# Second mixture: x stored to the output first, expert rows added onto it by the scatters, no closing stage

## The chip, the cores and the metric

The kernel runs on one core of one Trainium2 chip. The metric is the device time of one execution in microseconds; the time before is the median of three runs. A profile is of one execution. TensorE (PE), VectorE (DVE), ScalarE (ACT), Pool (GpSimd) and SP (SyncE) are the core's five engines; SP, ScalarE and Pool also issue the transfers (DMAs), which 16 DMA engines carry out.

## What is computed

3327 tokens of 256 features (padded to 26 tiles of 128 rows) go through four layers, each added onto `x`: a graph layer with an adjacency matrix, a mixture of experts, a second graph layer, and a transformer layer whose second half is another mixture. That last step is what the change is about:

```
def _moe(xf, ...):                      # capacity = ceil(T * 1.6 / 8)
    _, topk_idx = top_k(softmax(xf @ router_w + router_b), 2)
    out = zeros_like(xf)
    for i in range(8):
        sel = first `capacity` tokens that chose expert i
        hi = gelu(xf[sel] @ w1[i] + b1[i])
        out = out.at[sel].set(hi @ w2[i] + b2[i])     # a later expert overwrites
    return out
...
x = x + ctx @ wo + bo
h2 = layernorm(x)
return x + _moe(h2)
```

A token keeps the result of the last expert that took it, unweighted. A token that no expert took gets nothing. So each token has at most one expert row, and the result is `x` plus that row.

## The kernel before

The program is a list of blocks: first graph layer, routes and experts of the first mixture, second graph layer, attention, `second_norm`, routes and experts of the second mixture, and a closing block. All engines meet in a barrier at the end of each block; each engine first drains its own queue. Inside a block every engine has its instructions in the written order and waits on semaphores.

`second_norm` (line 1443) normalises `x` into `xhat`. SP stores `xhat` to `rows_d` in seven transfers (line 1559) and waits for them. Pool adds the kept `x` back onto `m.x` with seven transfers that add (line 1567, semaphore `back_added`); nothing in this block waits for these.

`mixture_routes` (line 638) is a chain of small VectorE operations: it picks the experts, ranks the tokens within each, and gives every token a slot among 20 chunks of 256 rows, each chunk of one expert. SP has nothing to do in it.

`expert_layers` (line 779) turns the slots into a list of token numbers (`index`, from which rows are gathered, and `place`, to which results go). Then, for each of the 20 chunks: Pool gathers 256 rows (two indirect transfers, line 1036), TensorE, ScalarE and VectorE compute the two layers with the chunk's weights, VectorE writes the result to one of two buffers `res` (line 1024), and Pool scatters it in two indirect transfers of 128 rows (line 1044). SP loads the weights two chunks ahead (line 841) and the biases (line 844). Pool's order in the loop is: gather chunk n+2, wait until the scatters of chunk n−1 landed and free that buffer (`release`), then wait for result n and scatter it. Slots without a token have a place of their own behind the 3328 rows.

The scatters write to `results1` in device memory. Tokens without an expert row must read zeros there, so Pool fills its first 3328 rows with zeros in the first graph layer (line 231, 13 transfers), behind the last use of the first four column groups of the adjacency matrix.

`mixture_output` (line 1068) is the closing block: SP reads the 3328 rows of `results1` in seven transfers (line 1079), VectorE multiplies each tile by the 0/1 weight of its tokens and adds it onto `x` (line 1087), ScalarE issues seven stores to `out` (line 1094) and waits for them.

Of the kernel before, what the change touches and what calls it, by code (L numbers as in the profile page):

```python
# [112 lines left out]
PIECE_RING = 4  # L113
RAW_RING = {True: 5, False: 4}
TOGETHER = 4
ZERO_TILES = 2
# [33 lines left out]
def graph_layer(nc, m, t, s, first):  # L150
# [38 lines left out]
    if first:  # L189
        made, params_loaded, x_loaded = s("made"), s("params_loaded"), [s(f"x_loaded{n}") for n in range(len(X_GROUPS))]  # L190
        rows_loaded, summed, reduced = [s("rows_loaded0"), s("rows_loaded1")], s("rows_summed"), s("rows_reduced")
        clamped, clamp_rooted = s("degree_clamped"), s("clamped_rooted")
        zero_made, rows_kept = s("zero_made"), s("rows_kept")
        m.pool_dma.append(rows_kept)
    else:
        wide_loaded, normed2, biased = s("qkv_loaded"), s("tiles_normed2"), s("bias_added")
        come, added = [s(f"row_come{n}") for n in range(GOT)], s("row_added")
        lifted = s("qk_lifted")
        x_kept, qk_kept, split = [s("x_kept0"), s("x_kept1")], [s("qk_kept0"), s("qk_kept1")], s("qk_split")
        m.pool_dma.extend(qk_kept + come)  # L200
    with ExitStack() as ctx:
# [9 lines left out]
        xt = sb("xt", [P, 2, KT, P])  # L211
        if first:
            adj_rows = m.xhat[:].rearrange("p t d -> p (t d)").rearrange("p (r n) -> p r n", r=2)
            zeros, iota_i, deg_tmp = sb("zeros", [P, ZERO_TILES, D]), sb("iota_i", [P, P], I32), sb("deg_tmp", [P, 2, NT])
# [9 lines left out]
        def _(pool):  # L224
            if first:
                make_constants(pool, m, iota_i, made)
                pool.memset(zeros[:], 0.0).then_inc(zero_made, 1)
                pool.wait_ge(zero_made, 1)
                pool.wait_ge(used, PIECES * TOGETHER)
                for n in range(0, NT, ZERO_TILES):  # L230
                    pool.dma_start(m.results1[0:NP, :].rearrange("(p n) d -> p n d", p=P)[:, n:n + ZERO_TILES, :], zeros[:]).then_inc(rows_kept, 16)
                for c in range(CHUNKS):
                    at = slice(first_tile(c), first_tile(c + 1))
                    pool.wait_ge(normed, at.stop)
                    pool.dma_start(m.rows_d[at.start * P:at.stop * P, :].rearrange("(k p) d -> p k d", p=P), m.xhat[:, at, :]).then_inc(rows_kept, 16)
# [399 lines left out]
            dve.wait_ge(chain, NT)  # L635


def mixture_routes(nc, m, s, bias, top, capacity, chunks, slot_sets, weights, idle_pool=None):

# [3 lines left out]
    with ExitStack() as ctx:  # L643
# [132 lines left out]

def expert_layers(nc, m, t, s, layer, chunks, n_rows, results):

# [20 lines left out]
    with ExitStack() as ctx:  # L801
# [229 lines left out]
        def _(pool):  # L1031
# [33 lines left out]
            release(chunks - 1)  # L1065


def mixture_output(nc, m, s, results, weight, x, out, x_whole):

    come, added, put = [s(f"results_come{c}") for c in range(CHUNKS)], s("results_added"), s("out_stored")
    with nc.sbuf_tensor(named("got"), [P, NT, D], F32) as got, nc.Block() as block:  # L1073

        @block.sync
        def _(sp):
            for c in range(CHUNKS):
                at = slice(first_tile(c), first_tile(c + 1))
                sp.dma_start(got[:, at, :], results[at.start * P:at.stop * P, :].rearrange("(k p) d -> p k d", p=P)).then_inc(come[c], 16)  # L1079

        @block.vector
        def _(dve):
            dve.wait_ge(*x_whole)
            for c in range(CHUNKS):
                dve.wait_ge(come[c], 16)
                for k in chunk_tiles(c):
                    dve.scalar_tensor_tensor(x[:, k, :], got[:, k, :], weight[:, k:k + 1], x[:, k, :], ALU.mult, ALU.add).then_inc(added, 1)  # L1087

        @block.scalar
        def _(act):  # L1090
            for c in range(CHUNKS):
                at = slice(first_tile(c), first_tile(c + 1))
                act.wait_ge(added, at.stop)
                act.dma_start(out[:, at, :], x[:, at, :]).then_inc(put, 16)
            act.wait_ge(put, 16 * CHUNKS)


def mixture(nc, m, t, s, layer, bias, capacity, chunks, results, out, idle_pool=None, x_whole=None):
    n_rows = TOP_K if capacity is None else 1
    mixture_routes(nc, m, s, bias, TOP_K, capacity, chunks, [(m.put[:, n, :], m.gets[n]) for n in range(n_rows)], m.weights, idle_pool)  # L1100
    expert_layers(nc, m, t, s, layer, chunks, n_rows, results)
    if out is not None:
        mixture_output(nc, m, s, results, m.weights[0], m.x, out, x_whole)


KEYS = 512
# [464 lines left out]
def second_mixture(nc, m, t, s, out):  # L1571

    back_added = second_norm(nc, m, s)
    mixture(nc, m, t, s, 1, m.bias8[:, 1, :], CAPACITY, MOE1_CHUNKS, m.results1, out, x_whole=(back_added, 16 * CHUNKS))


class Memory:


    def __init__(self, nc, ctx):  # L1580
# [23 lines left out]

        self.put = sb("put", [P, TOP_K, NT], I32)
        self.rows_d = dram("moe_rows", [NP, D])
        self.results0, self.results1 = dram("results0", [MOE0_CHUNKS * CHUNK, D]), dram("results1", [NP + MOE1_CHUNKS * CHUNK, D])
        self.x_kept, self.qk = dram("x_kept", [P, NT * D]), dram("qk_parts", [2, 2 * HG, P, NP])


def program(nc, t, out, phases="gnn0 moe0 gnn1 att moe1"):
    NAMES.clear()
    with ExitStack() as ctx:
# [15 lines left out]
        graph_layer(nc, m, t, s, True)  # L1629
        if "moe0" in phases:  # L1630
            _, s = stage()
            mixture(nc, m, t, s, 0, m.bias8[:, 0, :], None, MOE0_CHUNKS, m.results0, None,
                    idle_pool=lambda: nc.clear_and_free_semaphores([x for x in first if x not in m.pool_dma]))
        if "gnn1" in phases:
            _, s = stage()
# [56 lines left out]
```

## Time and profile before

| | us |
|---|---|
| median of three runs | 2770.12 |
| lowest, highest | 2769.33, 2773.91 |
| profiled execution, own time | 2769.95 |
| its span, first to last instruction | 2768.2 |
| busy in the span: TensorE | 2464.8 (89%) |
| busy in the span: VectorE, ScalarE, Pool | 2011.6, 1573.0, 1275.3 |
| second norm and routes | about 2407 to 2479 |
| experts of the second mixture | about 2479 to 2746 |
| closing block | 2746.0 to 2768.2 |

The page gives the busy time of each engine and 40 slices of the span. The last slice, 69 us long, shows TensorE at 5 tenths and the DMA engines at 4; slices are too coarse for the question here, so the rows below come from timelines and from the instructions of single lines. Queue instructions (DRAIN, EVENT_SEMAPHORE) belong to an engine's sequencer, marked by a q behind the engine's name.

### The profile page before, as it was taken

To read this page: it belongs to the slowest core of one execution; us is meant where nothing else is said; L and a number is where in the kernel's file an instruction comes from. 1 tells how busy PE (TensorE), PEld (TensorE's weight loads), DVE (VectorE), ACT (ScalarE), POOL (GpSimd) and SP (SyncE) were. 2 spreads that over 40 slices of the span, in tenths; PEclk is the share of its full clock that TensorE was granted. 3 is DMA by queue.
4 is the path that set the end of the run, shared out by engine and by line. 5 is a ranking of instruction groups with operands and counts; after the bars stand their busy time and mean duration, and the time that the engine had idled before them with its cause. 6 is when DMAs were issued, how large, how long until landed. Compare 5 with 4: busy or idle time off the path is not lost. (4 is left out here: it accounts for less than half of the span.)

```text
span 2768.2 us, 54324 instructions
## 1 busy us (share of the span) xinstructions
PE 2464.8 (89%) x20834; PEld 1910.6 (69%) x20834; DVE 2011.6 (73%) x3003; ACT 1573.0 (57%) x2642; POOL 1275.3 (46%) x752
## 2 busy tenths in 40 slices
PE   4879939999969998858999999999999999749995
PEld 3668839999968887734666666666666666449995
DVE  5775567888868866647777777777777777277885
ACT  4554426777745543314666666666666666536772
POOL 0001012222224302235888888888888888613331
PEclk9999969999989999977999999999999999859997
DMA  9987325666747754343000000040000000055674
GB/s 391 364 334 235 114 89 199 236 234 239 236 153 233 233 173 138 106 121 93 9 17 11 15 16 10 17 83 17 11 15 16 9 17 7 20 139 207 239 231 161
DMA packets 110608, 359.06 MB, mean 130 GB/s; under 512 B 21840, under 2 KB 48720, under 8 KB 93008
## 3 DMA queue, kind: packets, MB, share of 16 engines
q1 hardware_dynamic: 88528, 289.79, 30.6%
q0 software_dynamic: 19296, 58.48, 7.2%
q10 hardware_dynamic: 2592, 8.16, 0.7%
q8 instruction: 129, 2.11, 0.3%
q14 instruction: 63, 0.52, 0.1%
HBM read 311.80 MB, written 44.56 MB: 129 GB/s over the span
## 5 line engine op out<-in xcount | busy, mean ns | idle before, releaser
L1261 POOL TENSOR_TENSOR at_pool_sum<-at_pool_sum,at_probs 128x1024 f32<-128x1024 f32 x364 | 866.4, 2380 | 100.6 <-ACT at_probs L1387 59.8
L1416 DVE TENSOR_REDUCE at_part_max<-ps_x 128x2 f32<-128x1024 f32 x624 | 734.2, 1221 | 229.4 <-PE ps_x L1317 229.4
L1387 ACT ACTIVATE at_probs<-ps_s 128x512 f32<-128x512 f32 x1352 | 698.3, 603 | 325.3 <-PE ps_s L1276 302.6
L1276 PE MATMUL ps_s<-at_qst,at_kst 97*128 97x256 f32 x2704 | 518.1, 311 | 5.4 <-ACT at_probs L1387 4.3
L1276 PEld LDWEIGHTS ps_s<-at_qst,at_kst 97*128 97x128 f32 x2704 | 369.2, 190 | 219.1 <-ACT at_probs L1387 126.3
L1293 PE MATMUL ps_oz<-at_probs,k_xhat 128*32 128x256 f32 (+1 forms) x5408 | 392.2, 386 | 0.0
L483 PE MATMUL ps_acc<-adj_hi,y_hi 128*128 128x512 f32 (+1 forms) x728 | 289.0, 397 | 93.3 <-DVE adj_lo L549 61.5
L549 DVE TENSOR_TENSOR adj_lo<-adj_raw,adj_hi 128x1024 fp32r<-128x1024 f32 (+1 forms) x182 | 217.5, 1197 | 163.5 <-ACT adj_hi L325 161.3
L484 PE MATMUL ps_acc<-adj_lo,y_hi 128*128 128x512 f32 (+1 forms) x728 | 277.8, 382 | 0.0
L485 PE MATMUL ps_acc<-adj_hi,y_lo 128*128 128x512 f32 (+1 forms) x728 | 277.7, 381 | 0.0
L936 ACT ACTIVATE ex_hid<-ps_ex_h,ex_b 128x256 f32<-128x256 f32 x424 | 193.8, 476 | 124.4 <-PE ps_ex_h L877 114.7
L957 DVE TENSOR_TENSOR ex_w_lo<-ex_w,ex_w_hi 128x2048 fp32r<-128x2048 f32 x106 | 238.2, 2289 | 29.6 <-ACT ex_w_hi L918 29.6
L875 PE MATMUL ps_ex_h<-ex_rt_hi,ex_w_hi 128*128 128x256 f32 x848 | 241.3, 285 | 3.2 <-DVE ex_rt_lo L952 3.2
L875 PE MATMUL ps_ex_o<-ex_w_hi,ex_hid_hi 128*128 128x256 f32 x848 | 242.2, 286 | 0.0
L877 PE MATMUL ps_ex_h<-ex_rt_hi,ex_w_lo 128*128 128x256 f32 x848 | 238.5, 281 | 0.0
L876 PE MATMUL ps_ex_h<-ex_rt_lo,ex_w_hi 128*128 128x256 f32 x848 | 238.3, 281 | 0.0
L876 PE MATMUL ps_ex_o<-ex_w_lo,ex_hid_hi 128*128 128x256 f32 x848 | 238.0, 281 | 0.0
L877 PE MATMUL ps_ex_o<-ex_w_hi,ex_hid_lo 128*128 128x256 f32 x848 | 238.0, 281 | 0.0
L325 ACT ACTIVATE adj_hi<-adj_raw 128x1024 fp32r<-128x1024 f32 (+1 forms) x182 | 174.9, 988 | 102.8 <-PE ps_acc L485 99.8
L483 PEld LDWEIGHTS ps_acc<-adj_hi,y_hi 128*128 128x128 f32 x728 | 140.7, 193 | 126.4 <-issue 101.8
L1317 PE MATMUL ps_x<-at_keys,at_queries 32*128 32x512 f32 x1248 | 191.2, 511 | 26.7 <-DMA at_keys<-qk_parts 12.1
L1293 PEld LDWEIGHTS ps_oz<-at_probs,k_xhat 128*32 128x32 f32 (+1 forms) x5408 | 141.5, 109 | 105.0 <-issue 1.7
(226 smaller groups left out, 3981.5 us busy)
## 6 DMA issues: line engine op xcount, KB each, us to landing
ex_w<-w SPq DMA_DIRECT2D x106, 1024.0 KB, 7.7
adj_raw<-adjT SPq DMA_DIRECT2D x156, 512.0 KB, 4.7
k_xhat<-adj SPq DMA_DIRECT2D x26, 1664.0 KB, 7.7
at_qst<-qk_parts SPq DMA_DIRECT2D x78, 128.0 KB, 2.7
results<-ex_res POOLq DMA_DIRECT2D x33, 256.0 KB, 3.3
ex_b<-b SPq DMA_DIRECT2D x53, 128.0 KB, 2.3
adj_raw<-adjT_tail SPq DMA_DIRECT2D x26, 256.0 KB, 2.7
qk_parts<-qk_hi POOLq DMA_DIRECT2D x26, 256.0 KB, 2.8
```

The lines of the kernel that those rows point to most:

```text
L483: pe.matmul(out, y_hi[:, k, cols], hi[:, g % PIECE_RING, at], start=k == 0, stop=False)
L484: pe.matmul(out, y_hi[:, k, cols], lo[:, g % PIECE_RING, at], start=False, stop=False)
L485: last = pe.matmul(out, y_lo[:, k, cols], hi[:, g % PIECE_RING, at], start=False, stop=k == NT - 1)
L875: pe.matmul(out, hi, by_hi, start=start, stop=False)
L876: pe.matmul(out, hi, by_lo, start=False, stop=False)
L877: return pe.matmul(out, lo, by_hi, start=False, stop=stop)
L957: dve.tensor_tensor(w_lo[:, k, layer, :], w[:, k, layer, :], w_hi[:, k, layer, :].bitcast(F32), ALU.subtract).then_inc(weights_lo, 1)
L1261: pool.tensor_tensor(pool_sum[:, g % 2], pool_sum[:, g % 2], probs[:, tile % RING], ALU.add).then_inc(pool_added, 1)
L1276: last = pe.matmul(ps_s[:, unit % S_BANKS, hh, :], kst[:, 2 * j + hh, k * P:(k + 1) * P], qst[:, g % 2, 2 * j + hh, :], start=True, stop=True)
L1293: last = pe.matmul(ps_oz[h * DK:(h + 1) * DK, 0, :], m.xhat[0:rows, k, (hg * FOUR + h) * DK:(hg * FOUR + h + 1) * DK], probs[0:rows, tile ...
L1387: act.activation(probs[:, tile % RING, 2 * j:2 * j + 2], ps_s[:, unit % S_BANKS], ACT.Exp, scale=scale).then_inc(taken, 1)
L1416: dve.tensor_reduce(part_max[:, g % 2, heads, qt, kc], ps_x[:, pair, :], AX.X, ALU.max).then_inc(x_free, 1)
```

## The change

`x` is stored to `out` by one transfer on SP inside the block of the routes, behind a wait for `back_added`. The scatters of the second mixture go to `out` directly and add. Pool waits for the store of `x` before its first scatter. `results1`, its zeros and the closing block are removed; `out` gets the row layout and the extra rows that `results1` had, and the host cuts them off.

```diff
@@ graph_layer, Pool, first stage
-                pool.memset(zeros[:], 0.0).then_inc(zero_made, 1)
-                pool.wait_ge(zero_made, 1)
-                pool.wait_ge(used, PIECES * TOGETHER)
-                for n in range(0, NT, ZERO_TILES):
-                    pool.dma_start(m.results1[0:NP, :].rearrange("(p n) d -> p n d", p=P)[:, n:n + ZERO_TILES, :], zeros[:]).then_inc(rows_kept, 16)
...
-                pool.wait_ge(rows_kept, 16 * (CHUNKS + NT // ZERO_TILES))
+                pool.wait_ge(rows_kept, 16 * CHUNKS)
@@ mixture_routes
+        if keep_x:
+            @block.sync
+            def _(sp):
+                x_whole, out, x_stored = keep_x
+                sp.wait_ge(*x_whole)
+                sp.dma_start(out[0:NP, :].rearrange("(k p) d -> p k d", p=P), m.x[:]).then_inc(x_stored, 16)
@@ expert_layers, Pool
                         pool.indirect_dma_start(out=results, out_offset=bass.IndirectOffsetOnAxis(place[:, TT * n + a:TT * n + a + 1], 0),
-                                                in_=res[:, k, a, :], in_offset=None).then_inc(stored[k], 16)
+                                                in_=res[:, k, a, :], in_offset=None, compute_op=ALU.add).then_inc(stored[k], 16)
...
             if SPREAD:
                 pool.wait_ge(listed, 2)
+                pool.wait_ge(x_stored, 16)
@@ mixture_output: removed whole
-        def _(sp):
-            for c in range(CHUNKS):
-                sp.dma_start(got[:, at, :], results[at.start * P:at.stop * P, :].rearrange("(k p) d -> p k d", p=P)).then_inc(come[c], 16)
...
-                    dve.scalar_tensor_tensor(x[:, k, :], got[:, k, :], weight[:, k:k + 1], x[:, k, :], ALU.mult, ALU.add).then_inc(added, 1)
...
-                act.dma_start(out[:, at, :], x[:, at, :]).then_inc(put, 16)
@@ kernel
-    out = nc.dram_tensor("out", (P, NT, D), F32, kind="ExternalOutput").ap()
+    out = nc.dram_tensor("out", (NP + MOE1_CHUNKS * CHUNK, D), F32, kind="ExternalOutput").ap()
```

On SP, from the stores of the second norm (line 1559) through the routes to the weight loads of the experts, there stood before:

```order
L1559 DMA moe_rows<-k_xhat 128x4x256 [waits ln2_rows_made_146] x6
L1559 DMA moe_rows<-k_xhat 128x2x256 [waits ln2_rows_made_146]
L1451 UNCONDITIONAL_BRANCH [waits ln2_rows_kept_147]
L835 UNCONDITIONAL_BRANCH [waits barrier_Pool_Activation_PE_DVE_SP_release]
L846 UNCONDITIONAL_BRANCH
L846 ISA
L839 ISA [waits ex_weights_lo_164]
L839 TENSOR_LOAD k_owner
```

and now (the same stores are at line 1531):

```order
L1531 DMA moe_rows<-k_xhat 128x4x256 [waits ln2_rows_made_145] x6
L1531 DMA moe_rows<-k_xhat 128x2x256 [waits ln2_rows_made_145]
L1423 UNCONDITIONAL_BRANCH [waits ln2_rows_kept_146]
L759 UNCONDITIONAL_BRANCH [waits barrier_Pool_Activation_PE_DVE_SP_release]
L763 DMA out<-k_x 128x26x256 [waits ln2_back_added_151]
L637 UNCONDITIONAL_BRANCH
L836 UNCONDITIONAL_BRANCH [waits barrier_Pool_Activation_PE_DVE_SP_release]
L847 UNCONDITIONAL_BRANCH
L847 ISA
L840 ISA [waits ex_weights_lo_164]
```

The transfer `out<-k_x` has come in between the barrier that opens the routes and the one that closes them; the first weight load stands behind it.

On Pool, at the start of the expert block of the second mixture, before:

```order
L1451 UNCONDITIONAL_BRANCH
L1030 UNCONDITIONAL_BRANCH [waits barrier_Pool_Activation_PE_DVE_SP_gather]
L1036 DMA ex_rows<-moe_rows,ex_index 128x256 [waits ex_listed_178]
L1036 DMA ex_rows<-moe_rows,ex_index 128x256 x3
L1036 DMA ex_rows<-moe_rows,ex_index 128x256 [waits ex_turned_160,ex_listed_178]
L1036 DMA ex_rows<-moe_rows,ex_index 128x256
L1044 DMA results<-ex_res,ex_place 8448x256 [waits ex_out_made_170]
L1044 DMA results<-ex_res,ex_place 8448x256
L1036 DMA ex_rows<-moe_rows,ex_index 128x256 [waits ex_turned_160]
```

and now:

```order
L1423 UNCONDITIONAL_BRANCH
L1031 UNCONDITIONAL_BRANCH [waits barrier_Pool_Activation_PE_DVE_SP_gather]
L1037 DMA ex_rows<-moe_rows,ex_index 128x256 [waits ex_listed_178]
L1037 DMA ex_rows<-moe_rows,ex_index 128x256 x3
L1037 DMA ex_rows<-moe_rows,ex_index 128x256 [waits ex_turned_160,x_stored_152,ex_listed_178]
L1037 DMA ex_rows<-moe_rows,ex_index 128x256
L1045 DMA out<-ex_res,ex_place 8448x256 [waits ex_out_made_170]
L1045 DMA out<-ex_res,ex_place 8448x256
L1037 DMA ex_rows<-moe_rows,ex_index 128x256 [waits ex_turned_160]
```

The wait for `x_stored` sits on the third pair of gathers, together with two waits that were there. The scatters now name `out`.

On ScalarE, at the end of the program, before:

```order
L936 ACTIVATE ex_hid<-ps_ex_h,ex_b_109 128x256 [waits ex_hidden_lo_168,ex_hidden_ps_165]
L936 ACTIVATE ex_hid<-ps_ex_h,ex_b_109 128x256 [waits ex_hidden_ps_165]
L801 UNCONDITIONAL_BRANCH
L1089 UNCONDITIONAL_BRANCH [waits barrier_Pool_Activation_PE_DVE_SP_release]
L1094 DMA out<-k_x 128x1024 [waits results_added_189] x6
L1094 DMA out<-k_x 128x512 [waits results_added_189]
L1073 UNCONDITIONAL_BRANCH [waits out_stored_190]
```

and now:

```order
L937 ACTIVATE ex_hid<-ps_ex_h,ex_b_108 128x256 [waits ex_hidden_lo_168,ex_hidden_ps_165]
L937 ACTIVATE ex_hid<-ps_ex_h,ex_b_108 128x256 [waits ex_hidden_ps_165]
L937 ACTIVATE ex_hid<-ps_ex_h,ex_b_108 128x256 [waits ex_hidden_lo_168,ex_hidden_ps_165]
L937 ACTIVATE ex_hid<-ps_ex_h,ex_b_108 128x256 [waits ex_hidden_ps_165]
L802 UNCONDITIONAL_BRANCH
```

The barrier behind the expert block is the last; the seven stores and the block around them are gone.

## Rows read from the trace of the kernel before

**Rows 1.** Timeline of the end; columns: start us, us, engine line op tiles xcount [idle <-releaser].

```profile
2734.49 0.69 DVE L1024 TENSOR_TENSOR ex_res<-ps_ex_o,ex_b 128x512 f32<-128x512 f32 x1 [3.85 <-PE ps_ex_o L877]
...
2736.73 0.97 POOL L1044 DMA_INDIRECT results<-ex_res,ex_place  x1 [0.30 <-issue]
2746.05 5.70 SPq L1079 DMA_DIRECT2D got<-results  x7
...
2751.89 14.20 ACTq L1094 DMA_DIRECT2D out<-k_x  x7
```

**Rows 2.** Chain of waits that ended last; start us, us, what.

```profile
2750.33 14.48 DMA got<-results
```

**Rows 3.** Queue instructions of line 801; ns min/median/max, first to last start us.

```profile
L801 POOLq DRAIN  x2: 1288/3932/6575, 810.8 to 2739.2; - x2
L801 SPq EVENT_SEMAPHORE  x2: 17/17/17, 812.2 to 2746.0; - x2
```

**Rows 4.** Queue instructions of line 1451, where the second norm ends.

```profile
L1451 POOLq DRAIN  x1: 7212/7212/7212, 2441.9 to 2441.9; - x1
...
L1451 SPq EVENT_SEMAPHORE  x1: 17/17/17, 2452.5 to 2452.5; - x1
```

**Rows 5.** Queue instructions of line 1073, where the program ends.

```profile
L1073 POOLq DRAIN  x1: 46/46/46, 2746.0 to 2746.0; - x1
...
L1073 SPq EVENT_SEMAPHORE  x1: 17/17/17, 2768.2 to 2768.2; - x1
```

**Rows 6.** Timeline of Pool in the expert loop, one chunk.

```profile
2525.31 0.99 POOL L1044 DMA_INDIRECT results<-ex_res,ex_place  x1 [6.48 <-DVE ex_res L1024]
...
2529.82 0.97 POOL L1036 DMA_INDIRECT ex_rows<-moe_rows,ex_index  x1 [0.30 <-issue]
2536.91 1.07 POOL L1044 DMA_INDIRECT results<-ex_res,ex_place  x1 [6.12 <-DVE ex_res L1024]
```

**Rows 7.** DMA queues, 2440 to 2480 us: packets, MB, share of 16 engines.

```profile
q0 software_dynamic: 297, 0.79, 12.3%
q1 hardware_dynamic: 1299, 1.28, 9.3%
```

**Rows 8.** DMA queue of Pool, 2735 to 2768 us.

```profile
q0 software_dynamic: 96, 0.26, 2.2%
```

**Rows 9.** Transfers k_x<-x_kept of the second norm.

```profile
L1567 POOL DMA_DIRECT2D k_x<-x_kept x7: 850/852/947, 2414.4 to 2442.0; - x7
...
DMA to landing us min/median/max: 5.6/5.7/7.5
```

**Rows 10.** Transfers moe_rows<-k_xhat of the second norm.

```profile
DMA to landing us min/median/max: 2.9/4.0/6.2
```

**Rows 11.** Transfers results<-ex_res of the second mixture.

```profile
DMA to landing us min/median/max: 2.4/3.1/4.5
```

**Rows 12.** Stretches: us, then PE, PEld, DVE, ACT, POOL busy, PEclk, DMA share, GB/s.

```profile
2453.00:2479.00 26.00, 3.50 (x8) 2.34 (x8) 18.97 (x73) 1.22 (x2) 0.00 (x0) 0.50 0.00 0
2500.00:2735.00 235.00, 234.39 (x1987) 234.04 (x1985) 197.59 (x237) 163.31 (x226) 79.06 (x72) 0.99 0.60 209
```

**Rows 13.** Transfers ex_w<-w of the second mixture.

```profile
DMA to landing us min/median/max: 4.9/7.7/10.3
```

**Rows 14.** Timeline of SP: first weight load, and one in the loop.

```profile
2479.91 0.86 SPq L841 DMA_DIRECT2D ex_w<-w  x2
...
2527.86 0.81 SPq L841 DMA_DIRECT2D ex_w<-w  x2
```

**Rows 15.** Timeline of ACT: rounding of the weights loaded at 2527.86 us.

```profile
2541.35 3.71 ACT L918 ACTIVATE ex_w_hi<-ex_w 128x2048 fp32r<-128x2048 f32 x2
```

**Rows 16.** Timeline of Pool in the first graph stage.

```profile
226.65 7.24 POOL L231 DMA_DIRECT2D results<-zeros  x13 [222.23 <-PE ps_acc L485]
```

**Rows 17.** Waits, 215 to 250 us: total us, times, longest.

```profile
ACT adj_hi L325 <- PE ps_acc L485: 15.5, 9, 4.3
...
PE ps_acc L427 <- DVE gnn_tmp L557: 0.6, 1, 0.6
```

More of the change, by code:

```diff
@@ L192, in graph_layer @@
         clamped, clamp_rooted = s("degree_clamped"), s("clamped_rooted")
-        zero_made, rows_kept = s("zero_made"), s("rows_kept")
+        rows_kept = s("rows_kept")
         m.pool_dma.append(rows_kept)
@@ L213, in graph_layer @@
             adj_rows = m.xhat[:].rearrange("p t d -> p (t d)").rearrange("p (r n) -> p r n", r=2)
-            zeros, iota_i, deg_tmp = sb("zeros", [P, ZERO_TILES, D]), sb("iota_i", [P, P], I32), sb("deg_tmp", [P, 2, NT])
+            iota_i, deg_tmp = sb("iota_i", [P, P], I32), sb("deg_tmp", [P, 2, NT])
         else:
@@ L635, in _, with mixture_routes @@
             dve.wait_ge(chain, NT)
-def mixture_routes(nc, m, s, bias, top, capacity, chunks, slot_sets, weights, idle_pool=None):
+def mixture_routes(nc, m, s, bias, top, capacity, chunks, slot_sets, weights, idle_pool=None, keep_x=None):
     c_act, c_dve, c_pe = s("route_exp"), s("route_dve"), s("route_sums")
@@ L775, in _, with expert_layers @@
                 pe.matmul(ps[:, 1, 0:W], m.ones[:], flat, start=True, stop=True).then_inc(c_pe, 1)
-def expert_layers(nc, m, t, s, layer, chunks, n_rows, results):
+def expert_layers(nc, m, t, s, layer, chunks, n_rows, results, x_stored):
     loaded = [s("expert_loaded0"), s("expert_loaded1")]
@@ L1065, in _, with mixture @@
             release(chunks - 1)
[L1068 to L1075, printed above, removed]
-        def _(sp):
-            for c in range(CHUNKS):
-                at = slice(first_tile(c), first_tile(c + 1))
-                sp.dma_start(got[:, at, :], results[at.start * P:at.stop * P, :].rearrange("(k p) d -> p k d", p=P)).then_inc(come[c], 16)
[L1081 to L1086, printed above, removed]
-                    dve.scalar_tensor_tensor(x[:, k, :], got[:, k, :], weight[:, k:k + 1], x[:, k, :], ALU.mult, ALU.add).then_inc(added, 1)
[L1089 to L1093, printed above, removed]
-                act.dma_start(out[:, at, :], x[:, at, :]).then_inc(put, 16)
-            act.wait_ge(put, 16 * CHUNKS)
-def mixture(nc, m, t, s, layer, bias, capacity, chunks, results, out, idle_pool=None, x_whole=None):
+def mixture(nc, m, t, s, layer, bias, capacity, chunks, results, idle_pool=None, x_whole=None):
     n_rows = TOP_K if capacity is None else 1
[L1100 to L1103, printed above, removed]
+    x_stored = s("x_stored") if x_whole else None
+    mixture_routes(nc, m, s, bias, TOP_K, capacity, chunks, [(m.put[:, n, :], m.gets[n]) for n in range(n_rows)], m.weights, idle_pool,
+                   x_whole and (x_whole, results, x_stored))
+    expert_layers(nc, m, t, s, layer, chunks, n_rows, results, x_stored)
 KEYS = 512
@@ L1573, in second_mixture @@
     back_added = second_norm(nc, m, s)
-    mixture(nc, m, t, s, 1, m.bias8[:, 1, :], CAPACITY, MOE1_CHUNKS, m.results1, out, x_whole=(back_added, 16 * CHUNKS))
+    mixture(nc, m, t, s, 1, m.bias8[:, 1, :], CAPACITY, MOE1_CHUNKS, out, x_whole=(back_added, 16 * CHUNKS))
 class Memory:
@@ L1631, in program @@
             _, s = stage()
-            mixture(nc, m, t, s, 0, m.bias8[:, 0, :], None, MOE0_CHUNKS, m.results0, None,
+            mixture(nc, m, t, s, 0, m.bias8[:, 0, :], None, MOE0_CHUNKS, m.results0,
                     idle_pool=lambda: nc.clear_and_free_semaphores([x for x in first if x not in m.pool_dma]))
@@ L1687 @@
     t = {n: nc.dram_tensor(n, a.shape, F32, kind="ExternalInput").ap() for n, a in arrays.items()}
-    out = nc.dram_tensor("out", (P, NT, D), F32, kind="ExternalOutput").ap()
+    out = nc.dram_tensor("out", (NP + MOE1_CHUNKS * CHUNK, D), F32, kind="ExternalOutput").ap()
     program(nc, t, out)
     r = run_bass_kernel_spmd(nc, [arrays], core_ids=[0])
-    return r.results[0]["out"].transpose(1, 0, 2).reshape(NP, D)[:TOKENS]
+    return r.results[0]["out"][:TOKENS]
```

3 lines of the change are left out of this document (1 added, 2 removed).

## The prediction

> **What bounds the kernel now.** I read the page first: TensorE is busy 89% of the span, so most of the 2768 us is its work, and the change does not touch it. So I asked which part of the span the edited code owns. The timeline of the end answers [rows 1]: the last expert result is made at 2734.49 us, its second scatter is issued on Pool at 2736.73, and from then on no engine computes until the closing block. SP starts its loads at 2746.05, and ScalarE spreads the output stores over 14.20 us from 2751.89. The chain of waits [rows 2] contains only this block: 14.48 us of it is the last `got<-results` transfer. The program ends at 2768.2 [rows 5]. The closing block is therefore bound by 6.8 MB of transfers, with everything else idle.
>
> The 9 us between the last scatter and 2746 are not named by the chain, so I looked at the queue instructions of line 801, which ends the expert block. Pool's DRAIN there lasts 6575 ns from 2739.2, and the barrier frees SP at 2746.0 [rows 3]; the 1288 ns in the same row is the first mixture, where the last result is stored by a plain transfer. The last two scatters landed at most 4.5 us after issue, median 3.1 [rows 11], and Pool reached the drain at 2739.2, 2.5 us after issue; so the drain comes behind the landing.
>
> **The closing block goes.** The last barrier is now that of the expert block. Before, it freed SP at 2746.0 [rows 3] and the one of the closing block at 2768.2 [rows 5]: 22.2 us less, all of it on the path. Gone with it are 7 loads, 26 VectorE additions and 7 stores. The drain of the expert block stays: the code still ends that block with a barrier which Pool joins. The drain of the closing block was 46 ns [rows 5] and saves nothing.
>
> **The store of x.** It is one transfer of 3.41 MB on SP, in the block of routes, behind a wait for the 7 adding transfers. The last of these is issued at 2442.0 and lands at most 7.5 us later [rows 9], at 2449.5; SP is freed at 2452.5 [rows 4], so the wait costs nothing. The routes run from there without a single transfer: DMA share 0.00 from 2453 to 2479 [rows 12]. How long does it take? Plain transfers of SP moved 1.28 MB in 9.3% of 40 us, 344 GB/s [rows 7], which gives 9.9 us, end at 2462.5. The other bound is seven transfers of a seventh each, one after the other, at 4.0 us [rows 10]: 28 us, end at 2480.5, 0.6 us into the first weight load at 2479.91 [rows 14]. I take the first, since the row counts the engines' busy time on the same rows of 1 KB, and cost it at 0; its cover is the VectorE chain of the routes, and without it the 9.9 us would stand on the path. What is queued behind it on SP is only the barrier and the weight loads. Pool's new wait for the store stands before its third pair of gathers, in the block behind the routes, which end at 2479 [rows 12], and is met by then: 0. With the 28 us bound, 0.6 us.
>
> **Forty scatters become adding scatters.** The profile has no scatter that adds, but it has transfers that add: `k_x<-x_kept`. Two rows bound the price.
> - Engine time. Pool's queue moved 0.79 MB of additions in 12.3% of 40 us, 160 GB/s [rows 7]; the last two plain scatters moved 0.26 MB in 2.2% of 33 us, 361 GB/s [rows 8]. One scatter of 0.131 MB thus goes from 0.36 to 0.82 us.
> - Landing. 512 KB with addition took 5.7 us, without it 4.0 [rows 9, 10]: at most 1.7 us more for four times the bytes.
>
> In the loop the extra is 40 × 0.46 = 18 us of the DMA engines in 235 us, which lifts their share from 0.60 [rows 12] to 0.68. TensorE is busy 234.39 of 235 us there [rows 12], so only a delay of what it waits for counts. Weights: the pair issued at 2527.86 is rounded at 2541.35 [rows 14, 15], 13.5 us later; loads land in 10.3 us at worst [rows 13], so 3.2 us are left and the cost is 0. Pool: per chunk its period is 11.6 us; the chunk's transfers are issued by 2530.79, 5.5 us after 2525.31, and then it has 6.1 us to wait for the landing before the next store [rows 6]. The second scatter is issued 1.3 us into the chunk (0.97 us for the first, 0.30 between them [rows 1]), so it may land up to 10.3 us after issue. 3.1 + 1.7 is far below: 0.
>
> At the end there is no cover. The last addition has to land before Pool drains: +0.46 by engine time, +1.7 by landing. I take 1.0, between the two, as the smaller size speaks for the first and the read of the destination for the second. The drain is kept at 6.6 us: the one in the trace that stands behind an adding transfer is 7.2 us [rows 4], though it covers that transfer's landing too. Its bounds are 1.3 us (5.3 less) and double (6.6 more), and I keep both for the range.
>
> The Trainium skill, "DMA: Bandwidth & Descriptors", section "Anatomy of one DMA — SWDGE (gpsimd) path", gives a DMA about 2.0 us plus bytes/436e3 us, most of the fixed part being the receipt of the write, after which the semaphore fires. For 128 KB that would be an estimated 2.3 us, and the smallest landing in [rows 11], 2.4 us, agrees; but it knows no time behind the semaphore, and the 6.6 us drain is what the trace has on top. By the page alone the program would end near 2739.4 us; that result is the first rival.
>
> **The zero stores of the first stage go.** 13 transfers on Pool at 226.65 us and a fill before them [rows 16]. In 215 to 250 us ScalarE waits for TensorE, 15.5 us in 9 waits, and TensorE's own wait is 0.6 us for VectorE; no transfer is among the releasers [rows 17]. The zeros take bandwidth that nobody misses: 0, and at best those 0.6 us. Pool's `moe_rows` stores behind them wait for later tiles anyway.
>
> **Sum.** Profiled execution 2769.95 us, of which 2768.2 are span and 1.75 lie around it. 2769.95 − 22.2 + 0 + 0 + 1.0 = 2748.75 us. The profiled execution lies 0.17 us below the median of before (2770.12), so I forecast 2748.8 us, own range 2746 to 2753.
>
> **Rivals.**
> - The end comes earlier: nothing, or little, stands behind the last landing. For it: the 1.3 us drain of the first mixture, also an expert block. Against: scatters end both the old and the new block. With a drain of 1.3 us the time is 2748.8 − 5.3 = 2743.5; with none, 2768.2 is replaced by 2739.2 plus 0.2 for the barrier, plus 1 for the addition: 2742.2. Chance 0.10. The page named above would put it near 2741.2.
> - The tail grows: an adding scatter makes the drain longer. For it: the drain depends on the kind of the last transfer, 1.3 against 6.6 us, and nobody knows why. If it doubles, 2748.8 + 6.6 = 2755.4. Chance 0.12.
> - Weights come late: the larger DMA share stretches weight loads beyond 13.5 us after issue. Worst landing 10.3; with 14.6 us on each of 18 loads, TensorE loses 1.1 × 18 = 20 us, and the gain is gone: 2769. Against: the median is 7.7 [rows 13]. Chance 0.03.
> - Slower: Pool's release of the result buffer. It waits for the landing of a chunk's scatters before it stores the next, and VectorE may not overwrite the buffer until then. If the adding scatter needs more than 10.3 us, the period of every chunk becomes 1.3 us plus that landing, and TensorE starves after the two buffers are used. At 11.4 us the 19 chunks lose 21 us and the gain is gone; at 12 us, 19 × 1.7 = 32 us: 2781. For it: it would be row by row, a read and a write each at scattered addresses. Against: 512 KB of additions landed in 7.5 us at worst [rows 9]. Chance 0.04.
>
> **How the numbers follow.** The forecast has 0.71, the rivals 0.10, 0.12, 0.03 and 0.04. I count 0.2% of the time, 5.5 us, as what can be told from no change. The first three cases are faster by more: 0.93. Weights late gives the same, 0.03; Pool's release is slower, 0.04. The range runs from the middle of the early end to the doubled drain: 2742 to 2756.
>
> **What would show it.** In the new profile: last barrier at about 2747 us of span; Pool's drain of the last block 6 to 7 us and started 3 to 4 us after the last scatter; `out<-k_x` as one transfer that lands before 2465; DMA share near 0.68 in the expert loop with TensorE still full; the loop's Pool rows 11.6 us apart. The prediction is wrong if the distance between chunks grows, if ScalarE waits for `ex_w`, or if that drain is of another size than 6.6 us by more than 3.

## The result, and the profile after

The changed kernel takes 2749.1 us (median of 4 runs, 2743.97 to 2751.21) where the kernel before took 2770.92 us beside it (4 runs, 2769.33 to 2773.91). The ratio is 0.9915, 95% interval 0.9903 to 0.9928: 21.8 us less, against 21.3 forecast. The profiled execution took 2749.84 us, its span is 2748.1 us.

The timeline of the end of the kernel after, which answers to [rows 1] (start us, us, engine, line, operation, tiles, idle before and its releaser):

```profile
2737.04 0.28 PE L878 MATMUL ps_ex_o<-ex_w_hi,ex_hid_lo 128*128 128x256 f32 x1
2737.41 0.69 DVE L1025 TENSOR_TENSOR ex_res<-ps_ex_o,ex_b 128x512 f32<-128x512 f32 x1 [3.85 <-PE ps_ex_o L878]
2738.37 1.55 POOL L1045 DMA_INDIRECT out<-ex_res,ex_place  x1 [6.22 <-DVE ex_res L1025]
2740.23 1.55 POOL L1045 DMA_INDIRECT out<-ex_res,ex_place  x1 [0.30 <-issue]
```

Nothing computes behind these rows. The queue instructions of line 802, which now ends the program, answer to [rows 3] and [rows 5] (ns min/median/max, first to last start in us; the first of each pair is the first mixture):

```profile
L802 POOLq DRAIN  x2: 1288/2502/3717, 812.3 to 2744.1; - x2
...
L802 SPq EVENT_SEMAPHORE  x2: 17/17/17, 813.7 to 2748.0; - x2
```

The drain is 3.7 us, not the 6.6 of [rows 3]. From the start of the last scatter to the barrier are 7.8 us; before they were 9.3 (2736.73 to 2746.0). But the two scatters now take Pool 1.55 us each where they took 0.97, so the second one starts 2.8 us behind the start of the last addition, not 2.2. From the start of that addition to the barrier it was 11.5 us before and is 10.6 us after.

The adding scatters as a group (ns min/median/max), and their landing; this answers to [rows 11]:

```profile
L1045 POOL DMA_INDIRECT out<-ex_res,ex_place x40: 1549/1627/2089, 2516.9 to 2740.2; - x40
...
DMA to landing us min/median/max: 3.8/7.6/11.1
```

That is 7.6 us at the median and 11.1 at most, where a plain scatter took 3.1 and 4.5. What Pool makes of it, in its timeline (one chunk, for [rows 6]) and in its waits from 2500 to 2735 us (total us, times, longest):

```profile
2528.24 1.62 POOL L1045 DMA_INDIRECT out<-ex_res,ex_place  x1 [5.15 <-DVE ex_res L1025]
2530.16 1.62 POOL L1045 DMA_INDIRECT out<-ex_res,ex_place  x1 [0.30 <-issue]
2532.09 1.23 POOL L1037 DMA_INDIRECT ex_rows<-moe_rows,ex_index  x1 [0.31 <-PE ps_ex_t L872]
2533.63 0.98 POOL L1037 DMA_INDIRECT ex_rows<-moe_rows,ex_index  x1 [0.30 <-issue]
2540.99 1.62 POOL L1045 DMA_INDIRECT out<-ex_res,ex_place  x1 [6.38 <-DMA out<-ex_res,ex_place]
```

```profile
POOL out L1045 <- DVE ex_res L1025: 56.3, 11, 14.4
POOL out L1045 <- DMA out<-ex_res,ex_place: 53.3, 8, 7.5
```

Before, Pool's scatters waited only for VectorE there. Now they wait for a landing 8 times: the scatter issued at 2530.16 holds up the next store until 2540.99, 10.8 us later. The first scatters of successive chunks stood 11.8 us apart before; now they are mostly 13 and 10.5 us apart in turn, with the same mean over the loop (11.66 us). TensorE does not notice, as the stretches show, for [rows 12] (us; PE, PEld, DVE, ACT, POOL busy; clock, DMA share, GB/s):

```profile
2453.00:2479.00 26.00, 5.55 (x19) 4.29 (x18) 17.39 (x66) 2.04 (x3) 0.00 (x0) 0.50 0.40 131
...
2500.00:2735.00 235.00, 233.84 (x1978) 233.70 (x1978) 197.80 (x237) 164.16 (x227) 105.71 (x74) 0.99 0.71 213
```

The first of them holds the store of x, one transfer on SP:

```profile
2455.94 0.38 SPq L763 DMA_DIRECT2D out<-k_x  x1
```

It landed 11.3 us later, 16 us ahead of the first weight load at 2483.30. Pool's DMA queue from 2500 to 2735 us has twice the packets and 22.6% of the 16 engines; the same stretch of the kernel before had 3552 packets and 13.0%:

```profile
q0 software_dynamic: 7250, 9.84, 22.6%
```

**Where the time went, block by block.** The barriers at the ends of blocks, on SP, cut both executions into stages (us). The two columns on the right are profiles of the same two kernels taken later (e6 and e5):

| block | before | after | before again | after again |
|---|---|---|---|---|
| first graph stage | 366.6 | 367.8 | 367.2 | 365.0 |
| first mixture, routes | 21.3 | 21.3 | 21.3 | 21.3 |
| first mixture, experts | 423.6 | 423.9 | 423.3 | 423.4 |
| second graph stage | 413.1 | 417.4 | 417.5 | 413.7 |
| attention | 1181.5 | 1179.1 | 1180.7 | 1181.0 |
| second norm | 45.7 | 45.7 | 45.7 | 45.6 |
| second mixture, routes | 26.2 | 26.2 | 26.2 | 26.2 |
| second mixture, experts | 267.3 | 265.9 | 267.6 | 266.6 |
| closing block | 22.2 | none | 20.9 | none |

The second graph stage varies between 413 and 418 us from execution to execution in either kernel, without an edit in it; so a single pair of executions can be 4 us off. The expert block and the closing block are where the kernels differ.

### The profile page after: what moved, and what is told of

The parts are those of the page before. It is cut to its first block and busy times, and to the rows that moved or that the text cites. A ratio compares the mean times of both kernels' runs of the same rounds, so it can differ in the third digit from the quotient of the medians.

```text
span 2748.1 us, 54258 instructions
## 1 busy us (share of the span) xinstructions
PE 2467.7 (90%) x20834; PEld 1914.0 (70%) x20834; DVE 2001.7 (73%) x2977; ACT 1572.5 (57%) x2642; POOL 1294.0 (47%) x738
## 5 line engine op out<-in xcount | busy, mean ns | idle before, releaser
L1248 PEld LDWEIGHTS ps_s<-at_qst,at_kst 97*128 97x128 f32 x2704 | 369.3, 190 | 218.1 <-ACT at_probs L1359 125.7
```

Of the source, the lines that this page charges most:

```text
L1248: last = pe.matmul(ps_s[:, unit % S_BANKS, hh, :], kst[:, 2 * j + hh, k * P:(k + 1) * P], qst[:, g % 2, 2 * j + hh, :], start=True, stop=True)
```

## The experiments

They ran in three series; the kernel before ran in each. In the first series it took 2804.67 us (11 runs), in the second 2771.4 (15 runs), in the third 2772.51 (11 runs). The records name chip 13 for the first two and chip 9 for the third. The kernels below are compared within their series.

### First series

**e1: the adding scatter alone, in the kernel before.**

```
-  in_=res[:, k, a, :], in_offset=None).then_inc(stored[k], 16)
+  in_=res[:, k, a, :], in_offset=None, compute_op=ALU.add).then_inc(stored[k], 16)
```

> The kernel before with one edit: the scatters of the second mixture add onto the zeroed rows. Closing block and zeros stay. Theory (the adding itself is free in the loop and changes only the tail): TensorE stays full, and the last scatter to the barrier goes from 9.3 us to the 7.8 us seen in the changed kernel, so 2770.9 - 1.5 = 2769.4. Rival (the additions cost in the loop, and the closing block was worth more than 22 us): 2772 to 2776.

Measured: 2778.73 us (2776.02 to 2781.24), ratio 0.9904 (0.989 to 0.9918). Adding made the kernel before 26 us faster in this series. Both scatters move the same rows; this was not foreseen in the prediction. Its expert block lasted 266.7 us with 11.8 us a chunk, the drain behind it 3.7 us, the closing block 20.9.

**e2: the kernel after with plain scatters** (the output lacks x for each token with an expert row).

```
-  in_offset=None, compute_op=ALU.add).then_inc(stored[k], 16)
+  in_offset=None).then_inc(stored[k], 16)
```

> The changed kernel with scatters that overwrite instead of adding (tokens with an expert row get that row alone, without x). Theory: the drain of Pool depends on the kind of its last transfers, so it is back at 6.6 us, the landing shrinks from 3.9 to 2.5 us, and the end comes 1.5 us later than with additions: 2750.6; scatters land in 3.1 us median in the loop, with no effect on the time. Rival (the additions cost something on the path): 2745 to 2747.

Measured: 2784.91 us (2774.59 to 2791.13), ratio 0.992 (0.9904 to 0.9936). The profile is that of the slowest of the six executions. Its expert block took 301.2 us, and most chunks 13.6 to 14.0 us instead of 11.8. TensorE is no longer full; from 2500 to 2780 us:

```profile
2500.00:2780.00 280.00, 246.96 (x2000) 242.90 (x2000) 201.52 (x240) 164.17 (x228) 80.55 (x78) 0.96 0.53 183
```

The waits of the same stretch name VectorE's `ex_w_lo`, and waits put down to `issue` or `remote`, which name no instruction as releaser:

```profile
PEld ps_ex_h L876 <- issue: 30.1, 17, 2.1
PE ps_ex_h L876 <- DVE ex_w_lo L958: 23.2, 15, 1.9
...
ACT ex_hid L937 <- remote: 14.6, 13, 1.6
```

And ScalarE's timeline shows where a chunk loses its 2 us: the last two activations come 1.6 us late each, one behind VectorE's `ex_hid_lo` and one behind `remote`; the rounding of the next weights is late with them, and then TensorE waits.

```profile
2593.65 0.47 ACT L937 ACTIVATE ex_hid<-ps_ex_h,ex_b 128x256 f32<-128x256 f32 x1 [0.15 <-issue]
2595.68 0.47 ACT L937 ACTIVATE ex_hid<-ps_ex_h,ex_b 128x256 f32<-128x256 f32 x1 [1.55 <-DVE ex_hid_lo L1018]
2597.76 0.48 ACT L937 ACTIVATE ex_hid<-ps_ex_h,ex_b 128x256 f32<-128x256 f32 x1 [1.61 <-remote]
...
2598.61 3.71 ACT L919 ACTIVATE ex_w_hi<-ex_w 128x2048 fp32r<-128x2048 f32 x2
```

So in this series plain scatters cost 26.6 us by the medians (against e3) and 34.7 us by the profiled expert blocks. e1, which differs from the kernel before in the kind of scatter alone, is 25.9 us faster than it; so the same loss would explain the 2804.67 us of the kernel before here, though no profile of it was taken in this series. About 10 of the 35 us are TensorE working slower: its 2026 matmuls of the block took 249.1 us where the kernel after has 239.4, and after a stretch in which it was busy for 2.2 of 4 us (2600 to 2604) its granted clock was 0.61 and then 0.53 until 2608. The DMA engines were less busy, not more (0.53). Whether this belongs to the plain scatter was asked again in the third series.

**e3: the kernel after with the zero stores of the first stage put back** (13 transfers of zeros into a table that nobody reads, and the fill before them).

```
+  pool.memset(zeros[:], 0.0).then_inc(zero_made, 1)
+  pool.wait_ge(zero_made, 1)
+  pool.wait_ge(used, PIECES * TOGETHER)
+  for n in range(0, NT, ZERO_TILES):
+      pool.dma_start(m.results1[0:NP, :]...[:, n:n + ZERO_TILES, :], zeros[:])...
```

> The changed kernel with the zero stores of the first stage put back (into a buffer that nobody reads). Theory: they are hidden, 2749.1 within 0.6 us, and the first stage ends at the same time. Rival: they cost bandwidth in the first stage, and part of the 21.8 us came from them: 2751 to 2755.

Measured: 2758.36 us (2754.56 to 2760.24), ratio 0.983 (0.9817 to 0.9842). Its first stage lasted 366.2 us. Over all profiles that stage is 366.2 to 369.3 us in the four with zeros and 364.6 to 367.9 us in the ten without: the means are 1.2 us apart, less than the spread within either group, so that these cannot tell the cost of the zeros from nothing. The more telling comparison is with e1, which has the same zeros and the same adding scatters and differs in where x goes: 2778.73 less 2758.36 is 20.4 us, and e1's closing block is 20.9 us.

**e4: the store of x behind the routes**, ahead of the first weight load on SP.

```
-  (in the block of routes) sp.dma_start(out[0:NP, :]..., m.x[:]).then_inc(x_stored, 16)
+  (in the expert block, before load(0, 0)) sp.wait_ge(*x_whole); the same transfer
```

> The changed kernel with the store of x moved from the block of the routes to the start of the expert block, on SP ahead of the first weight load. Theory: the store (11.3 us to landing) was hidden only by the routes. Here it shares the DMA engines with the first weights and the first gathers, so TensorE's first chunk starts up to 10 us later: 2755 to 2759. Rival (the first chunk waits for something else, or the transfers interleave so that the weights lose little): 2749 to 2752.

Measured: 2760.21 us (2757.79 to 2763.66), ratio 0.9843 (0.983 to 0.9855). By time it cannot be told from e3 (1.9 us of medians); the profile can: the expert block lasted 273.8 us where e3's lasted 266.5, and those of all other kernels with one adding scatter for each 128 rows and no fill behind them lasted 264.1 to 266.7. In the two profiled executions other stages, which the edit doesn't touch, differ by about as much the other way (attention 1185.0 us in e3, 1181.2 in e4). ScalarE's first rounding of weights in this kernel, and in e3:

```profile
2503.52 3.71 ACT L923 ACTIVATE ex_w_hi<-ex_w 128x2048 fp32r<-128x2048 f32 x2 [13.43 <-DMA ex_w<-w]
```

```profile
2500.54 3.71 ACT L925 ACTIVATE ex_w_hi<-ex_w 128x2048 fp32r<-128x2048 f32 x2 [3.11 <-DMA ex_w<-w]
```

It waits 13.4 us for the weights instead of 3.1, since the 3.3 MB of x are ahead of them. The cover that the prediction named is real: without it the store costs some 7.3 us in that block. That figure rests on profiles alone; the whole times show 1.9 us of it.

### Second series

**e5: the kernel after itself.**

> The kernel after itself, on another chip than the first comparison, in one series with the kernel before. Theory A (the gain is the closing block alone): the expert blocks of both kernels run at the same 11.8 us a chunk, and the distance is again 21 to 23 us. Rival (plain scatters can stall the expert loop on some chips): here the loop of the kernel before has periods of 13.9 us, as the earlier look at plain scatters had, and the distance is 22 plus about 26 us, some 45 to 50 us; the kernel after has 11.8 us a chunk either way.

Measured: 2749.63 us (2745.34 to 2750.28), ratio 0.9919 (0.9906 to 0.9933). The gain is 21.8 us again, with 11.8 us a chunk. The kernel before took 2771.4 us. The records give this series the same chip number as the first, so the 26 us of the first series don't belong to a chip, contrary to how the expectation put it.

**e6: the kernel before itself, for its profile.**

> The kernel before itself, for its profile on this chip. Theory A: its expert block lasts 267 us with 11.8 us a chunk, as in its first profile. Rival: about 300 us with 13.9 us a chunk, since it scatters plainly. If the chip is one where the kernel before takes 2770 us, theory A's number is expected of both.

Measured: 2772.91 us; expert block 267.6 us, closing block 20.9. Plain scatters, 11.8 us a chunk: the first theory's number.

**e7: Pool fills a spare buffer between the last landing and its drain.**

```
   release(chunks - 1)
+  if SPREAD:
+      pool.memset(m.xhat[:], 0.0).then_inc(res_free, 1)
+      pool.wait_ge(res_free, chunks + 3)
```

> Pool fills the buffer xhat with zeros (nobody reads it any more) after it has seen the last scatters land and ahead of its last drain; the fill is 6144 elements a partition and should take 5 to 13 us. Theory A: the 3.7 us of the drain at the end are work of Pool's queue that starts when the last transfer has landed and runs beside Pool's engine; then the drain behind the fill falls to below 1.5 us and the time rises by the fill less about 3 us. Theory B: the drain is work that begins only when Pool reaches it; then it stays at 3 to 4 us and the time rises by the whole fill. In both the landing of the last scatters stays near 4 us.

Measured: 2752.35 us (2751.48 to 2758.09), ratio 0.9937 (0.9923 to 0.995). The end on Pool, and its queue's drain:

```profile
2737.12 1.55 POOL L1045 DMA_INDIRECT out<-ex_res,ex_place  x1 [0.30 <-issue]
2740.80 5.65 POOL L1069 MEMSET k_xhat<- 128x6656 f32 x1 [2.13 <-DMA out<-ex_res,ex_place]
```

```profile
L802 POOLq DRAIN  x2: 1288/2506/3724, 809.9 to 2746.6; - x2
```

The drain starts 5.8 us later and lasts 3.7 us all the same. From the start of the first of the last two scatters to the barrier it is 15.2 us instead of 9.6, the whole fill. (The fill is 6656 elements a partition, not the 6144 of the expectation.) The whole times agree only roughly: 2.7 us more than e5 by medians, 5.3 by means. So the drain is work that begins when Pool reaches it; it doesn't run down beside other work of Pool.

**e8: each adding scatter issued twice**, the second time into a scratch table; the release waits for all four.

```
+  pool.indirect_dma_start(out=m.spare_rows, out_offset=..., in_=res[:, k, a, :],
+                          in_offset=None, compute_op=ALU.add).then_inc(stored[k], 16)
-  pool.wait_ge(stored[n % 2], (n // 2 + 1) * (32 if SPREAD else 16))
+  pool.wait_ge(stored[n % 2], (n // 2 + 1) * (64 if SPREAD else 16))
```

> Each adding scatter is issued twice, the second time into a scratch table, so that four adding transfers stand in Pool's queue for a chunk, and the result buffer is released when all four have landed. Theory A (the release of the result buffer is nearly used up in the kernel after: landings of 7.6 us median and 11.3 at most against 10.3 us of margin): the period of a chunk grows from 11.8 to between 13.4 and 17 us, TensorE waits, and the time rises by 34 to 103 us. Rival (the queue overlaps the four, and the release still has room): period stays at 11.8, time rises by under 8 us, at the tail alone.

Measured: 2772.41 us (10 runs, 2765.59 to 2785.07), ratio 0.9999 (0.9989 to 1.0009): 22.8 us more than e5, and the whole gain of the change is gone. The profiled execution was the slowest of the ten. Its expert block lasted 302.6 us; the additions of VectorE that end the chunks stood 11.3 to 22.0 us apart, but for the last. The waits from 2500 to 2780 us, and Pool's rows of one stretch:

```profile
PEld ps_ex_t L872 <- DMA ex_rows<-moe_rows,ex_index: 24.4, 6, 8.6
POOL out L1045 <- DMA spare_rows<-ex_res,ex_place: 18.0, 8, 3.0
```

```profile
2571.97 1.74 POOL L1045 DMA_INDIRECT out<-ex_res,ex_place  x1 [2.44 <-DMA spare_rows<-ex_res,ex_place]
2574.02 1.75 POOL L1047 DMA_INDIRECT spare_rows<-ex_res,ex_place  x1 [0.30 <-issue]
2576.07 3.17 POOL L1045 DMA_INDIRECT out<-ex_res,ex_place  x1 [0.30 <-issue]
2579.55 1.89 POOL L1047 DMA_INDIRECT spare_rows<-ex_res,ex_place  x1 [0.30 <-issue]
2581.74 1.26 POOL L1037 DMA_INDIRECT ex_rows<-moe_rows,ex_index  x1 [0.30 <-issue]
```

The direction is the one of the first theory, at less than its price (34 to 103 us) by the medians, though the profiled block is 36.7 us longer than in the kernel after. But the way there is another. No wait of VectorE for a free result buffer is among the waits; TensorE waits for the gathered rows of the next chunk, whose issue stands behind the scatters in Pool's queue. The gathers themselves landed as fast as in the kernel after (median 6.1 us, at most 9.5, for 6.7 and 8.9). So Pool's slowness reaches TensorE through what Pool issues next. (The expectation's landing of 11.3 us was that of the store of x; the scatters of the kernel after took 11.1 at most.)

The waits for rows are 24.4 of the 36.7 us. Another 8.7 us are TensorE's own work, which runs slower behind such a wait: the 2026 matmuls of the block kept it busy for 248.1 us instead of 239.4. The longest wait, 8.4 us, ended at 2592.85; the granted clock was 0.50 behind it, the lower of its two levels, and 1.00 again from 2600 (columns as in [rows 12]):

```profile
2585.00:2590.00 5.00, 0.00 (x0) 0.00 (x0) 1.28 (x3) 0.00 (x0) 4.39 (x3) 0.87 0.97 298
2590.00:2595.00 5.00, 2.15 (x10) 2.15 (x11) 0.37 (x1) 1.00 (x2) 4.06 (x4) 0.50 1.08 261
2600.00:2605.00 5.00, 5.00 (x47) 5.00 (x46) 2.80 (x4) 1.83 (x4) 1.80 (x2) 1.00 0.10 27
```

### Third series

**e9: SP instead of Pool waits for the last landing.**

```
-  release(chunks - 1)
+  if not SPREAD:
+      release(chunks - 1)
   ... (sync)
+  if SPREAD:
+      sp.wait_ge(stored[(chunks - 1) % 2], ((chunks - 1) // 2 + 1) * 32)
```

> SP instead of Pool waits for the landing of the last two scatters, so that Pool reaches its drain right behind the issue of the last scatter. Theory B (the drain is a fixed 3.7 us of work that starts when Pool reaches it, as the run with the fill on Pool has it): it now runs beside the landing, starts some 2 us earlier after the last issue, lasts 3.7 us again, and the distance from the last scatter's issue to the last barrier falls from 7.8 to about 5.7 us; time 1.5 to 2.5 us below the kernel after. Rival (the drain also covers whatever is still under way): it lasts 5.8 us or more, the distance stays 7.8 us and the time stays.

Measured: 2750.44 us (2747.82 to 2753.98), ratio 0.9923 (0.991 to 0.9936), not to be told from e12. The queue instructions at the end:

```profile
L802 POOLq DRAIN  x2: 1288/5062/8837, 813.3 to 2743.2; - x2
L802 SPq EVENT_SEMAPHORE  x2: 17/17/17, 814.7 to 2752.2; - x2
L802 SPq COMPARE_BRANCH  x1: 38/38/38, 2748.7 to 2748.7; - x1
```

SP is through its wait at 2748.7, 3.7 us after the last scatter started (2745.01): the landing. The record of the drain now starts with the issue of the scatters and ends at 2752.0, 3.3 us behind the landing. From the last scatter to the barrier it is 7.2 us, against 7.8: 0.6 us gained, not 2. So the rival holds, but for those 0.6 us: the drain doesn't end before what is under way has landed, and ends some 3.3 us behind it. Whether it waits and then works, or works slower beside the transfers, the record doesn't tell apart.

**e10: in addition, the last chunk half by half.**

```
+  for a in range(TT):            # the last chunk on TensorE: all of half 0, then half 1
+      for h in range(HT):
+          last = three(ps_o[:, a, 0:D], ...)
+      last.then_inc(out_ps if a else half_ps, 1)
   ... (vector) one addition for each half, (gpsimd) a wait before each scatter
```

> The same, and the last chunk's output matmuls are done for the first 128 rows and then for the second, with the bias addition and the scatter of the first half issued while TensorE works on the second. Of the tail one issue (1.55 + 0.30 us) goes too. Expected: from the last matmul to the last barrier 2.1 + 1.9 + about 0.2 us (the addition covers half the elements) less than in the kernel after, which has 10.7 us; time about 4 us below the kernel after, near 2745.5 us where the kernel after takes 2749.6. Rival: the two issues stand one after the other on Pool anyway, because the first half is finished less than 1.9 us before the second, and the gain is 2 us.

Measured: 2747.2 us (2740.82 to 2749.81), ratio 0.9908 (0.9894 to 0.9922), the lowest of all, though e12 is within its interval. The end in its timeline:

```profile
2738.02 1.55 POOL L1071 DMA_INDIRECT out<-ex_res,ex_place  x1 [3.27 <-DVE ex_res L1039]
...
2739.63 0.28 PE L881 MATMUL ps_ex_o<-ex_w_hi,ex_hid_lo 128*128 128x256 f32 x1
2739.94 0.42 DVE L1041 TENSOR_TENSOR ex_res<-ps_ex_o,ex_b 128x256 f32<-128x256 f32 x1 [2.20 <-PE ps_ex_o L881]
2740.83 1.55 POOL L1071 DMA_INDIRECT out<-ex_res,ex_place  x1 [1.25 <-DVE ex_res L1041]
```

The first half is scattered while TensorE works on the second. From the last matmul (2739.63) to the barrier (2747.9) it is 8.3 us, against 11.0 in the kernel after (2737.04 to 2748.0), and the expert block is 264.1 us against e12's 266.6. That is 2.5 to 2.7 us of the 4 expected; the missing part is about what was missing in e9. A gain of this size is shown by the profile and not by the times.

**e11: plain scatters once more** (the same kernel as e2).

> Plain scatters in the changed kernel once more (the output then lacks x for every token with an expert row), to see whether the 13.9 us a chunk of the first series belongs to the plain scatter or to the conditions of that series, in which the kernel before itself took 2804 us. The records give both earlier series the same chip number, so it is not a matter of the chip. If the kernel before takes about 2771 us in this series: 11.8 us a chunk here, an expert block of 266 to 268 us, and a time within 4 us of the kernel after (it has the longer drain, 6.6 against 3.7 us, and the shorter issue and landing). If the kernel before takes about 2804 us: 13.9 us a chunk again. If the chunk takes 13.9 us while the kernel before takes 2771, the plain scatter into the output table itself is to blame.

Measured: 2750.51 us (2744.09 to 2753.87), ratio 0.9927 (0.9915 to 0.9939). The kernel before took 2772.51 us in this series, and here the expert block lasted 266.9 us with 11.8 us a chunk. The landing is shorter and the drain longer than with adding scatters:

```profile
L802 POOLq DRAIN  x2: 1288/3932/6575, 808.5 to 2735.5; - x2
```

So in both later series plain scatters ran at 11.8 us a chunk, like adding ones (the second by e6, this one by e11), and the 13.9 us appeared only where the conditions of the first series and the plain scatter came together.

**e12: the kernel after itself.**

> The kernel after itself in this series, as the measure for the other three. 2747 to 2751 us where the kernel before takes 2771; if this series is like the first one, 2755 to 2762 us, with 11.8 us a chunk in the second mixture and about 12.05 in the first, while the kernel before takes 2804.

Measured: 2747.75 us (2746.08 to 2750.2), ratio 0.9918 (0.9905 to 0.9931); expert block 266.6 us. The gain is 24.8 us of medians; the intervals of the ratio overlap those of the other comparisons.

## Why the prediction was right, step by step

**The closing block.** Right. It gave −22.2 us in the first profile; the one taken again has 20.9, and e1 against e3 gives 20.4 in whole times. So the forecast took the highest of the values seen.

**The store of x.** Right, at 0. It took 11.3 us, near the 9.9 bound and far from the 28, and had 16 us to spare. e4 shows that the cover does the work: 7.3 us without it.

**The adding scatter in the loop.** The cost of 0 is right, with two sizes wrong. The engines' extra time was forecast at 18 us and is 9.6% of 235, 22.6 us: share 0.71 for 0.68. The landing was put "far below" 10.3 us, by 3.1 + 1.7 from a direct transfer that adds; it is 7.6 at the median and 11.1 at most, beyond the 10.3. The rival "Pool's release of the result buffer" was thus much nearer than its 0.04. A single late landing delays one store and the next chunk makes up for it, as the distances of 13 and 10.5 us show; that the two buffers and the early gathers are what gives this slack is read from the code, and no run varied them. e8 shows that the distance to the edge is less than a second pair of scatters. And there it struck through the gathers, not through VectorE as the rival had it. The Trainium skill, "DMA: Bandwidth & Descriptors", section "Anatomy of one DMA — SWDGE (gpsimd) path", would give an estimated 2.3 us for 128 KB; the shortest landing of an adding scatter is 3.8 us in the kernel after and 3.5 in any profile, so its formula doesn't hold for one that adds.

**The tail.** The step that failed, though its errors partly cancel and the time stayed near the forecast. The prediction put +1.0 us for the landing and kept the drain at 6.6. Measured: +0.6 for the longer issue of the first scatter, which the prediction forgot, +1.4 for the landing (3.9 for 2.5 us from the start of the last scatter to the start of the drain), and −2.9 for the drain (3.7 for 6.6). The sum is −0.9 where the forecast had +1.0. The bound of a drain of 1.3 us was too low, the bound of the doubled one too high. Why an adding scatter leaves a shorter drain than a plain one stays open; e7 and e9 show that it is neither a countdown from the last transfer nor the landing itself.

**The zeros.** Right at 0, as far as e3 can tell.

**Sum.** By these steps −22.2 − 0.9 = −23.1 us; the two profiled executions differ by 20.1. The 3.0 us between are spread over the other stages: +4.3 in the second graph stage, which varies from 413 to 418 us in either kernel, +1.2 in the first, +0.3 in the first mixture, −2.4 in the attention and −0.5 in the rest of the expert block. The edit touches only the first graph stage and the expert block among these. That 21.3 forecast and 21.8 measured agree to 0.5 us is partly luck: the wrong sign of the tail and the highest value of the closing block (22.2, against 20.9 in the later profile) offset each other. Two of the prediction's signs were missed: the drain was not 6 to 7 us, and the landing of the store fell at 2467.2 instead of before 2465, in a block that itself began 3.4 us later.

**What stays open** is the first series. The first mixture's block lasted 429.2 to 430.5 us in its four kernels, 423.3 to 424.9 in all others. In the second mixture plain scatters cost 2.1 us a chunk; adding ones cost nothing (266.5 to 266.7 us in e1 and e3), and they even landed sooner than elsewhere (medians 3.9 to 4.3 us in e1, e3 and e4, for 7.6 to 7.9 in the profiles of the same scatters outside this series). In e2 ScalarE's activations were late, in part behind waits for which the profile names no instruction. Nothing here tells why, and the gain there would have been about 46 us, counting e3 as the kernel after, rather than 22.

## What to carry to other kernels

A last stage that only moves and combines data can often be dissolved: store the one operand under a stage that leaves the DMA engines alone, and let the other be added by the transfers that write it anyway. The price to look at is not the extra bytes but the landing and the issue time on the queue, and what else that queue has to issue: count how far ahead its next loads are. A tail has fixed parts behind its last transfer (here 11 us from the last matmul), and what shortened it was an earlier last transfer (2.5 us in e10 with e9's edit, 0.6 for e9's alone) more than another engine that waits for it.

## What the hardware did that was not expected

- An adding scatter of 128 rows of 1 KB occupied Pool for 1.55 us at least and 1.63 at the median where a plain one took 0.97 and 1.07, and landed in 7.6 us at the median in the loop of the kernel after (3.9 to 4.3 in the first series), 3.6 to 3.8 us with nothing else under way, where the plain one took 3.1 and 2.5. Pool's queue, gathers included, had 7250 packets in 235 us where it had 3552.
- Pool's drain at a block's end had a length that depends on what it issued before, the same within 10 ns from run to run: 1288 ns behind plain transfers, 6575 behind plain scatters (four profiles), 3717 behind adding ones (six profiles; 3724 with the fill between), 2982 where each was issued twice. Where Pool didn't wait for the landing first, the record also covers it: 8837 in e9, 7130 in e10.
- A wait of TensorE cost more than its length: behind the 8.4 us in e8, which ended at 2592.85, the granted clock was 0.50 and only from 2600 us 1.00 again; the block's matmuls took 8.7 us more in all than in the kernel after.
- In one series plain scatters made each chunk of the loop some 2.1 us longer and adding ones did not; in two others both ran at 11.8 us.
